# Building the experts' row lists: marks written tile by tile with per-partition numbers instead of in groups of eight tiles

## The reference, cut to what matters

```python
# layer 0: two experts for each token
logits = x @ router_w.T
routing_weights, selected = sparsemixer_eval(logits, JITTER_EPS)      # first and second maximum
for e in range(E):
    h = silu(x @ w_gate[e].T) * (x @ w_up[e].T)
    out = out + dense_w[:, e:e + 1] * (h @ w_down[e].T)

# layer 1: one expert for each token
top_idx = argmax(gate_logits, axis=-1)
for e in range(NUM_EXPERTS):
    mask = (top_idx == e)[..., None]
    h = relu(x @ w1[e] + b1[e])
    out = out + mask * (h @ w2[e] + b2[e])
```

## Time and profile before

| what | value |
|---|---|
| median of three executions | 1180.13 us (1178.96 to 1181.77) |
| span of the profiled execution | 1175.1 us |
| own time of the profiled execution | not listed beside its span; the median is 5.0 us above the span |
| TensorE busy (matmul) | 878.0 us, 75% |
| VectorE busy | 887.3 us, 76%, 1790 instructions |
| ScalarE busy | 630.2 us, 54% |
| GpSimd busy | 738.3 us, 63% |

### The profile page before, as it was taken

One profiled execution on the slowest core, in us unless ns is written; L12 is line 12 of the kernel. 1 busy time (PEld: TensorE's weight loads), 2 busy tenths in 40 slices (PEclk: granted clock), 3 DMA queues, 4 the chain that ended last, 5 costly groups with the idle time before them and its releaser, 6 DMA issues. The chain is left out here.

```text
span 1175.1 us, 14982 instructions
## 1 busy us (share of the span) xinstructions
PE 878.0 (75%) x4244; PEld 565.5 (48%) x4244; DVE 887.3 (76%) x1790; ACT 630.2 (54%) x1401; POOL 738.3 (63%) x508
## 2 busy tenths in 40 slices
PE   7797769886987787753999736596987978349930
PEld 4243324334433433333999713264665767339920
DVE  4896999899979999966666555486896878465512
ACT  4787635874587465516343313656567684246710
POOL 0898799989988999702666376355433443037646
PEclk8999989998999898865999967598989977569975
DMA  6644445455544554340233312111101020142323
GB/s 185 184 131 131 125 147 166 137 157 160 162 131 143 164 164 156 113 164 13 71 85 87 72 50 68 45 34 50 45 2 64 28 74 19 54 165 73 71 63 98
DMA packets 90905, 118.95 MB, mean 101 GB/s; under 512 B 12508, under 2 KB 48804, under 8 KB 90696
## 3 DMA queue, kind: packets, MB, share of 16 engines
q1 hardware_dynamic: 84168, 104.34, 28.7%
q0 software_dynamic: 6656, 13.64, 5.0%
HBM read 103.70 MB, written 14.25 MB: 100 GB/s over the span
## 5 line engine op out<-in xcount | busy, mean ns | idle before, releaser
L687 POOL TENSOR_TENSOR ma_bu<-ma_u,ma_row_b 128x1024 f32<-128x1024 f32 x128 | 300.7, 2377 | 15.6 <-DVE ma_u L898 8.0
L416 PE MATMUL y_ps<-ma_h,ident 128*128 128x512 f32 x512 | 254.1, 635 | 27.4 <-POOL ma_h L697 23.1
L1215 POOL DMA_INDIRECT s_rows<-xs,take x112 | 128.9, 1151 | 162.3 <-POOLq L951 105.6
L563 ACT ACTIVATE decay_ps<-ma_delta,negA 128x512 f32<-128x512 f32 x256 | 172.5, 686 | 85.8 <-DVE ma_h L790 82.9
L416 PEld LDWEIGHTS y_ps<-ma_h,ident 128*128 128x128 f32 x512 | 100.4, 204 | 156.1 <-issue 111.1
L1568 POOL TENSOR_TENSOR mi_dec<-mi_dec,mi_gm 128x512 f32<-128x512 f32 x32 | 40.7, 1272 | 135.0 <-DVE mi_gm L2033 111.5
L1232 PE MATMUL s_up_ps<-s_xt,s_w 128*128 128x128 f32 x896 | 122.6, 282 | 1.2 <-ACT s_xt L1259 1.2
L780 DVE TENSOR_TENSOR_SCAN decay_ps<-decay_ps,ma_carry,ma_bu 128x512 f32<-128x512 f32 x88 | 110.1, 1271 | 12.6 <-issue 9.7
L790 DVE TENSOR_TENSOR ma_h<-decay_ps,ma_row_c 128x512 f32<-128x512 f32 x176 | 116.9, 665 | 0.0
L1232 PEld LDWEIGHTS s_up_ps<-s_xt,s_w 128*128 128x128 f32 x896 | 113.2, 198 | 1.6 <-DVE s_w L1291 1.0
L697 POOL TENSOR_TENSOR ma_h<-ma_h,ma_row_c 128x1024 f32<-128x1024 f32 x40 | 97.1, 2428 | 17.4 <-DVE ma_h L780 15.6
(11 more groups left out here) (323 smaller groups left out, 1766.0 us busy)
## 6 DMA issues: line engine op xcount, KB each, us to landing
ma_row_b<-bc_rows SPq DMA_DIRECT2D x128, 256.0 KB, 3.6
ma_row_c<-bc_rows SPq DMA_DIRECT2D x128, 256.0 KB, 3.3
mi_cs<-cs_rows SPq DMA_DIRECT2D x32, 256.0 KB
ys<-s_outs SPq DMA_DIRECT2D x28, 256.0 KB
w<-in_experts SPq DMA_DIRECT2D x1, 4112.0 KB, 14.9
w<-in_experts SPq DMA_DIRECT2D x1, 3072.0 KB, 10.3
xs<-rows SPq DMA_DIRECT2D x4, 512.0 KB, 3.4
out<-X SPq DMA_DIRECT2D x8, 256.0 KB
```

Source lines behind the costliest of these rows:

```text
L416: mm = pe.matmul(y_ps[:, j, :], m.ident[:], h[g % HS][:, j, :], start=False, stop=True, skip_group_check=True)
L563: act.activation(decay[s % DS][:], delta[b % 2][:, j, col(c)], ACT.Exp, scale=m.negA0[:, j, n:n + 1]).then_inc(decay_done, 1)
L687: pool.tensor_tensor(bu[g % BUS][:], u[b % 2][:, :, col(c)], both(row_b[g % BS]), ALU.mult).then_inc(bu_done, 1)
L1215: pool.indirect_dma_start(rows[s % ROWS][:], None, m.xs[layer], bass.IndirectOffsetOnAxis(ap=m.take[:, s:s + 1], axis=0)).then_inc(fetched ...
```

## The change

`in_slot` is written tile by tile, by one instruction that compares with the slot and multiplies by the token's number; both are now numbers of the partition (a column of 128 numbers, one for each partition). `at_spot` is written tile by tile too where VectorE does it. `slot`, `spot` and `m.ids` become 32-bit floats. The groups that ScalarE marks are the odd ones below 6: 1, 3 and 5 in layer 0 (five groups before) and 1 and 3 in layer 1 (as before). VectorE counts two for each group that it marks whole and one for the others.

```diff
-    by_act = [g for g in range(groups) if (g % 3 > 0 if layer == 0 else g % 2 == 1)]
-    own_marks = lambda g: sum(2 if q in by_act else 3 for q in range(g))
+    by_act = [g for g in range(groups) if g % 2 == 1 and g < 6]
+    own_marks = lambda g: sum(1 if q in by_act else 2 for q in range(g))
...
-        slot = sb("slot", [P, choices, TILES], F16)
-        spot = sb("spot", [P, choices, TILES], F16)
+        slot = sb("slot", [P, choices, TILES])
+        spot = sb("spot", [P, choices, TILES])
...
-                    before = marks + own_marks(of)
-                    A, B = [P, MARK, P], [P, MARK, slots]
-                    dve.tensor_tensor(in_slot[:, k, T, :], m.counth[:, 0:slots].unsqueeze(1).broadcast_to(B),
-                                      slot[:, k, T].unsqueeze(2).broadcast_to(B), ALU.is_equal).then_inc(marked, 1)
+                    for t in range(T.start, T.stop):
+                        ins = dve.tensor_scalar(in_slot[:, k, t, :], m.counth[:, 0:slots], slot[:, k, t:t + 1], m.ids[:, t:t + 1],
+                                                ALU.is_equal, ALU.mult)
+                    ins.then_inc(marked, 1)
                     if of not in by_act:
-                        dve.tensor_tensor(at_spot[:, k, T, :], m.counth[:].unsqueeze(1).broadcast_to(A),
-                                          spot[:, k, T].unsqueeze(2).broadcast_to(A), ALU.is_equal).then_inc(marked, 1)
-                    dve.wait_ge(marked, before + 1)
-                    dve.tensor_tensor(in_slot[:, k, T, :], in_slot[:, k, T, :], m.ids[:, T].unsqueeze(2).broadcast_to(B),
-                                      ALU.mult).then_inc(marked, 1)
+                        for t in range(T.start, T.stop):
+                            ins = dve.tensor_scalar(at_spot[:, k, t, :], m.counth[:], spot[:, k, t:t + 1], None, ALU.is_equal)
+                        ins.then_inc(marked, 1)
...
-        m.ids = sb("ids", [P, TILES], F16)
+        m.ids = sb("ids", [P, TILES])
...
-    arrays["ids"] = np.arange(-TOKENS // 2, TOKENS // 2).astype(mybir.dt.np(F16)).reshape(TILES, P).T.copy()
+    arrays["ids"] = np.arange(-TOKENS // 2, TOKENS // 2).astype(np.float32).reshape(TILES, P).T.copy()
```

## The result

The changed kernel takes 1186.72 us (median of 20 runs, 1180.09 to 1193.47), the kernel before 1182.0 us in as many (1171.69 to 1185.69). The ratio is 1.0039, with a 95% interval of 1.0022 to 1.0057: **slower by 4.7 us** between the medians, 2.6 to 6.7 us by the interval, 0.4% in all. Forecast were +6.0 us and 1186.1 us. Of all executions timed for this text one, in experiment 6, took 1378.79 us at a mean granted clock of 0.62 where the others had 0.84 to 0.86; it has no part in any ratio here.

A forecast was written before the change was run, and what follows sets the result against it. ScalarE was taken to set the end of both marking stretches, VectorE after the change. Layer 0 +3.4 and layer 1 +2.6 make +6.0 us; 1175.1 + 6.0 + 5.0 = 1186.1 us, own range 1183 to 1189, wider range up to 1195.

The forecast's parts named there:

- Who ends last: Both layers' marking to `take`: ScalarE sets the end before, VectorE 1.5 and 0.55 us ahead; VectorE ends last after.
- The steps: VectorE's narrow marks, start to start: `in_slot` 0.209 us in layer 0, 0.200 in layer 1; `at_spot` 0.156.
- Four at a time: VectorE's narrow marks: one-input 16-bit instructions go by the byte rate, four numbers at a time, 0.26 ns a column.
- What hides the products: Before `take`: TensorE's last eight products (0.64 us) lie beside the owners' steps and cost nothing; uncovered, 0.7 us.
- The waits and the split: Marking: the product's wait for the comparison goes, none is added; ScalarE loses two groups in layer 0, VectorE takes them.
- The 32-bit `slot`, `spot` and `ids`: Three conversions of 64 columns to another type and 8 KB more load: nothing, ends -0.1 to +0.1 us.
- The sum: Whole kernel: +3.4 us in layer 0 and +2.6 in layer 1, sum +6.0 us, giving 1186.1 us.
- What lies around the span: Outside the profiled span of 1175.1 us: left as it is, 5.0 us up to the median of the three.
- The faster rival: Marking: numbers per partition cost nothing in a run; layer 0's `take` 5.7 us sooner, time 1174.4 us; chance 0.10.
- The rival's other half: VectorE's narrow marks: a step is 0.07 us fixed and the columns, giving steps of 0.09 and 0.10.
- The slower rivals: Marking: 16 bits at two numbers a time, 1189.5 us, or one, 1196.3; kin, a step floor, 1192.9; chance together 0.28.
- No change: Marking: price half hidden, mean step 0.148 over all 152, 1180.1 us; chance, with gain or loss next to it, 0.12.

The follow-up runs named there:

- experiment 6: Kernel before, wide marks, a group's eight tiles innermost, ScalarE marking groups 1 and 4 (layer 1: 1): 1174.68 against 1175.86 us, ratio 0.9988; with ScalarE's old groups, untimed.
- experiment 4: Parts alone, start to `take` in layer 0 (before 18.21 us): split 18.74, narrow marks with old split 19.23; changed kernel with `in_slot` wide 19.57, `at_spot` wide 21.01.
- the set: Runs of narrow VectorE instructions on a scratch tile before layer 0's marking, changed kernel; on 72 columns, step 0.147 us with one number per partition, 0.209 with two.
- experiment 1: Changed kernel plus nine sets of narrow VectorE instructions before layer 0's marking; two-number steps 0.191, 0.209, 0.223 us for 8, 72, 128 columns; whole time not given.
- experiment 5: Kernel before, wide marks, ScalarE at three groups in layer 0, products with tokens' numbers on GpSimd: `take` at 20.63 us in layer 0, 7.72 in layer 1.

## Why the prediction was right

- *Who ends last.* I had ScalarE setting the end before, 1.5 and 0.55 us behind VectorE's own, and VectorE after. The brackets at `take` say the same, and in two runs of experiment 4 the first 1.50 us that VectorE's marking grew by left `take` where it was.
- *The steps.* 0.209 and 0.200 for `in_slot` against the 0.209 of the set and, in the changed kernel, (1.76 - 0.30) / 7 = 0.209 and (1.70 - 0.29) / 7 = 0.20; 0.156 for `at_spot` against (1.39 - 0.25) / 7 = 0.163. This last one is the small miss in layer 0: 40 x 0.007 = 0.3 us. It comes from 0.05 for the first number per partition, where the set has 0.058.
- *Four at a time.* Chosen against two and one at a time, without a row of a 16-bit instruction with one input; the choice went by the 32-bit rows, and experiment 1 bears it out. The 32-bit input in place made the marking longer by 2.5 and 0.9 us, which is the difference between four and two.
- *What hides the products.* Costed at nothing under the owners' steps, 0.7 without them; 0.84 and 0.63 measured.
- *The waits and the split.* VectorE has no idle time in brackets in its whole marking, as forecast. In the changed kernel TensorE's brackets name VectorE before each group and ScalarE nowhere. Costing the split inside VectorE's sum was right: it is 0.5 us by itself and 2.6 behind narrow marks.
- *The 32-bit `slot`, `spot` and `ids`.* Two conversions change their type, not three; they take 0.20 and 0.19 us in both kernels, so the term is nothing, as forecast.
- *The sum.* +6.0 forecast, 6.35 in the two stretches, 4.7 (2.6 to 6.7) in the whole. That 1186.1 lies within 0.6 us of 1186.72 is luck: the three runs that the forecast started from had a median 1.9 us under that of the 20, and the loss was forecast 1.3 us too large.
- *What lies around the span* was taken as 5.0 us, from the median. In executions whose span and time are both listed it is about 2 (1197.83 against a span of 1195.9). By that the profiled execution before took about 1177 us, an estimate, and was quicker than the median; the 5.0 holds both, and 1175.1 + 5.0 is nothing but the median of the three.

The faster rival fails on its mechanism: a number per partition costs its 0.06 us in a run of eight just as in the fours of the earlier trace rows. The rival's other half is true, 0.089 for an instruction without such numbers. The slower rivals fail on experiment 1: 128 columns of 16 bits cost 0.014 us more than 72, where two at a time would make it 0.029, and 8 columns are quicker than 72, so there is neither a slower rate nor a floor. No change would have needed a mean step of 0.148; (19.85 + 9.01) / 152 is 0.190.

## What to carry to other kernels

Price many small instructions by the step from start to start of a run of the same kind, with its operands, and not by busy time or by columns; then compare the sum with the engine's lead on the one that ends last, which here was 1.5 us. A wide instruction that broadcasts can be laid out so that the broadcast axis isn't the innermost, and this was worth more than any split tried here (11.79 us to `take` against 18.21 and 18.74); but check who else writes and reads the tile with the stride that this makes. Before work moves to an idle engine, ask what it shares with the busy one: GpSimd, idle in this stretch, made it 1.9 us longer (20.63 against 18.74 with the same split).

## What the runs showed of the hardware

- VectorE's comparison and product on two 16-bit inputs in which one is broadcast: 0.67 us a step for 576 columns with the broadcast innermost, 0.37 with it on the middle axis.
- ScalarE's 128x128 activations into 16-bit columns 16 bytes apart: eight in 4.90 us, in 2.44 when dense. TensorE's products from such operands: eight in 1.30 us against 0.66, at a granted clock of 0.50 both times, and in 1.20 when only the right operand, the one of 72 columns, has the stride.
- A number per partition costs VectorE's instruction on 72 16-bit columns 0.06 us each in the step from start to start: 0.089, 0.147 and 0.209 with none, one and two.
- GpSimd's product and VectorE's two-input comparisons ran one after the other: a comparison of 1.22 us took 2.16 (experiment 5).
- The stretch between the two markings, in which nothing differs in most of these kernels, took 484 to 497 us in single executions. Most of that lies in `middle`, 346.1 to 358.4 us from its first to its last instruction. What scatters there is open.
